# A projection's mask moved into VectorE's gated product, and the roots of its norm chains into one power on GpSimd

## Chip, cores and metric

The kernel runs on one core of a Trainium2 chip. The metric is device time in microseconds (us) of one execution; the median of three runs is given. The engines are TensorE (PE in the profile, its weight loads PEld), VectorE (DVE), ScalarE (ACT), GpSimd (POOL) and SyncE (SP, which here only issues DMAs).

## What is computed

A triangle-style pair update on a 192 x 192 grid with 128 channels, followed by a mixture of experts on the 36,864 tokens. The change touches only the first part, the projections:

```python
zn, pp, lp, ip = (_ln(t, ln_g, ln_b) for t in (z, protein_pair, l_pair, inter_pair))   # norms over 128 channels
gate_proj = lambda x, Wg, bg, W, b: sigmoid(x @ Wg + bg) * (x @ W + b)                  # 128 -> 64
ab1 = gate_proj(zn, Wg1, bg1, W1, b1) * z_mask[..., None]
ab2 = gate_proj(zn, Wg2, bg2, W2, b2) * z_mask[..., None]
ab3 = gate_proj(zn, Wg3, bg3, W3, b3) * z_mask[..., None]
pp, lp, ip = gate_proj(pp, 2), gate_proj(lp, 1), gate_proj(ip, 1)     # shortened: weights by number, no mask
block = einsum('bikc,bkjc->bijc', pp, ab1) + einsum('bikc,bjkc->bijc', ab2, lp) + ab3 * ip
```

z is itself the norm of x over its channels. A norm needs the reciprocal root of variance plus a small constant.

## The kernel before

Four phases run one after another: the projection (to about 547 us), the triangle products, a mix with norms, and the feed-forward. In the projection the grid is cut into 12 blocks of 16 rows; a block has 24 tiles of 128 positions x 128 channels for each of four inputs, x, pp, lp and ip. They are worked in four passes: x in 12 groups of two tiles (G = 0 to 11 of a block), pp, lp and ip in six groups of four tiles each (G = 12 to 17, 18 to 23, 24 to 29). Each engine runs its own program over the same 30 groups, and only semaphores tie them.

For a group, VectorE first takes mean and squares of its tiles (`stats_of`, L96, two tiles an instruction). From these a chain of small VectorE steps makes a scale and a shift for each tile (`chain_step`): a variance (L348), a reciprocal root in eight steps (`rsqrt_step`, L102 to L113), the shift (L352) and an addition (L354). There are two chains a block: EARLY holds the 56 tiles of pp, lp and the first third of ip, its steps standing three to a group from G = 4 on; LATE holds the rest of ip and the next block's x, 40 tiles (24 ahead of the first block, 16 in the last), from G = 17 on. Tables (`share_out`) say at which group each statistic and step stands.

Then the tiles are normalized in place three groups ahead of their use (`norm`): ScalarE takes one tile of a group, or two (L555), GpSimd the others (L594): one of an x group, two or three of the rest. TensorE transposes the tiles one group ahead (`turn`, L645), ScalarE copies the transposes out of PSUM (L566), TensorE projects them (L658) into one of three PSUM buffers, ScalarE applies the sigmoid to the gate half (L582, two buffers `sig_a`). In the x pass GpSimd now multiplies the gates by the mask (L615), and VectorE multiplies value by gate (L727); in the other passes VectorE multiplies at once (L733, L737). TensorE may project into a buffer only when the product of three groups before is done, and ScalarE may reuse a gate buffer only after the product of two groups before.

GpSimd also adds in ab3 * ip (`times_ab3`, L604), six a block: four in the ip pass, the last two in G = 0 and 1 of the next block's x pass, behind the mask product of that group. SP issues the loads of the next block's tiles as TensorE has turned the old ones, and the stores of the products: those of ab wait for the last product of the x pass, and the loads of pp for the next block stand behind them in SP's queue.

Of the kernel before, what the change touches and what calls it, by code (L numbers as in the profile page):

```python
# [22 lines left out]
P = 128  # L23
# [152 lines left out]
def setup_parts(nc, d, s, ctx, ps):  # L176
# [69 lines left out]
    def vector(dve):  # L246
# [16 lines left out]
        ins.then_inc(mask_made, 1)  # L263

# [47 lines left out]
CHAIN_STEPS = LN_STEPS + 1  # L312
# [17 lines left out]
share_out(COEFS_A, AT_X + 4, 3, EARLY, 0, range(CHAIN_STEPS))  # L330
share_out(STATS_A, AT_X + 8, 2, 3, 0, range(IP_SPLIT, TPB, 2))
share_out(STATS_A, AT_PP, 3, 0, 1, range(0, TPB, 2))
share_out(COEFS_A, AT_PP + 5, 3, LATE, 1, range(CHAIN_STEPS))
# [4 lines left out]
def chain_step(nc, dve, step, stepped, before, stats, work, parts, rstd, shift, ready):  # L338

    v = nc.vector  # L340
    tiles = stats.shape[1]
    var, t = (work[:, q, 0:tiles] for q in range(2))
    y = rstd
    if step > 0:
        dve.wait_ge(stepped, before + step)
    if step == 0:
        for lo, hi, factor, addend in parts:
            ins = v.tensor_scalar(var[:, lo:hi], stats[:, lo:hi, SQUARES], factor / CH, addend, ALU.mult, ALU.add)  # L348
    elif step < 1 + RSQRT_STEPS:
        ins = rsqrt_step(v, step - 1, y, t, var)  # L350
    elif step == LN_STEPS - 1:
        ins = v.scalar_tensor_tensor(shift, stats[:, :, MEAN], -1.0, y, ALU.mult, ALU.mult)  # L352
    else:
        v.tensor_scalar(shift, shift, 1.0, None, ALU.add).then_inc(ready, 1)  # L354
        return
    ins.then_inc(stepped, 1)
# [37 lines left out]
def project_phase(nc, d, s):  # L394


    with ExitStack() as ctx:
# [5 lines left out]
        work = sb("work_a", [P, 2, EARLY_TILES])  # L403
# [15 lines left out]
        coefs_ready, own, pool_passed = [sem("early_ready"), sem("late_ready")], sem("coef_stepped_a"), sem("pool_passed_a")  # L419
        q_made = sem("q_made")  # L420
        normed_act, normed_pool = sem("normed_act"), sem("normed_pool")
        turned, copied, projected = sem("turned"), sem("copied"), sem("projected")
        gated, masked, multiplied = sem("gated"), sem("masked"), sem("multiplied")
# [25 lines left out]
        def pool_tiles(i, t0, size):  # L449
            return list(range(t0 + act_share(i, t0), t0 + size))  # L450

# [140 lines left out]
        def _(pool):  # L592
# [29 lines left out]
            setup_gpsimd(pool)  # L622
# [1175 lines left out]
```

## Time and profile before

| | us |
|---|---|
| median of three runs (1394.88 to 1396.71) | 1395.43 |
| profiled execution | 1397.95 |
| its span, first to last instruction | 1396.2 |
| TensorE busy (95% of the span) | 1331.0 |
| VectorE / ScalarE / GpSimd busy | 1125.4 / 998.5 / 996.4 |

How the rows further down are read: in a row in order of time stand the start and the length in us, the engine, the line of the code, the operation, output <- input with shapes, and how many instructions are merged in the row; a bracket at the end is the engine's idle time before it and what ended that. "x8" of a projection are the halves of eight records, one group. In a row by stretches stand the stretch, its length, then the busy time of PE, PEld, DVE, ACT and POOL with the number of instructions, the granted clock of TensorE as a share of its upper level, the mean busy share of the DMA engines, and GB/s. In a row of groups stand line, engine, operation, tiles, shapes and count, then the total in us and the mean of one in ns, then the idle time before them and what ended it.

### The profile page before, as it was taken

Reading aid. Unit: us, or ns where it says so; the run is one execution under the profiler, and the core shown is the slowest. Engines: PE = TensorE matmul, PEld = TensorE weight load, DVE = VectorE, ACT = ScalarE, POOL = GpSimd, SP = SyncE. Lnnn points to the kernel's source line nnn. Section 1 sums busy time; section 2 is a strip of 40 time slices with the busy share of each in tenths; the row PEclk is TensorE's granted clock in tenths of the full one; section 3 lists DMA queues with packets and bytes.
Section 4 is the critical chain, followed back from the end, with each engine's and each line's share of the span. In section 5 each row is a group of like instructions: output and inputs, shape, how many; then the busy total and the mean of one; then the engine's idle time right before and its main releaser. Section 6 shows DMA issues by size and latency. Waiting matters only on the chain. (4 is left out here: it accounts for less than half of the span.)

```text
span 1396.2 us, 30985 instructions
## 1 busy us (share of the span) xinstructions
PE 1331.0 (95%) x9880; PEld 1129.6 (81%) x9880; DVE 1125.4 (81%) x2905; ACT 998.5 (72%) x2327; POOL 996.4 (71%) x1559
## 2 busy tenths in 40 slices
PE   6999999999999997999899999799999999999995
PEld 3887788777887777988767777699999999999994
DVE  6878778888888873787798887667888888888897
ACT  3888889888888886555477776346777766777773
POOL 4998999999999998444389888335555555555574
PEclk9999999999999998999999999899999999999998
DMA  9999999999999999888699994311222232222223
GB/s 214 226 256 258 250 248 249 259 262 257 241 251 267 263 238 291 282 303 294 182 298 333 320 320 172 99 37 61 77 76 76 77 89 79 76 76 77 77 61 91
DMA packets 357520, 267.40 MB, mean 192 GB/s; under 512 B 60432, under 2 KB 332722, under 8 KB 357362
## 3 DMA queue, kind: packets, MB, share of 16 engines
q1 hardware_dynamic: 355800, 264.76, 71.2%
q8 instruction: 82, 1.34, 0.4%
q10 hardware_dynamic: 1290, 0.46, 0.2%
q14 instruction: 76, 0.62, 0.2%
q0 software_dynamic: 272, 0.21, 0.1%
HBM read 171.02 MB, written 94.37 MB: 190 GB/s over the span
## 5 line engine op out<-in xcount | busy, mean ns | idle before, releaser
L1539 ACT ACTIVATE hT<-psH_d,b 128x512 f32<-128x512 f32 x288 | 197.4, 689 | 150.5 <-PE psH_d L1579 150.4
L658 PE MATMUL psZ_a<-w_all,xT_a 128*128 128x128 f32 x1728 | 230.2, 276 | 3.6 <-DVE ip_prod L737 2.0
L658 PEld LDWEIGHTS psZ_a<-w_all,xT_a 128*128 128x128 f32 x1728 | 209.8, 192 | 7.0 <-ACT xT_a L566 4.3
L658 PE MATMUL psZ_a<-w_all,xT_block 128*128 128x384 f32 x576 | 213.4, 493 | 0.1
L582 ACT ACTIVATE sig_a<-psZ_a 128x256 f32<-128x256 f32 (+1 forms) x360 | 153.8, 427 | 74.3 <-PE psZ_a L658 52.0
L594 POOL TENSOR_SCALAR shared<-shared,coefs_early 128x128 f32<-128x128 f32 x468 | 204.1, 461 | 0.0
L645 PE MATMUL psT_a<-ident,shared 128*128 128x128 f32 x1152 | 186.1, 274 | 4.6 <-issue 3.1
L1233 DVE TENSOR_SCALAR shared<-shared,coef 128x128 f32<-128x128 f32 x288 | 185.4, 703 | 1.6 <-POOL xh_b L1613 1.6
L645 PEld LDWEIGHTS psT_a<-ident,shared 128*128 128x128 f32 x1152 | 141.0, 142 | 56.1 <-issue 28.5
L1606 POOL TENSOR_TENSOR u_d<-u_d,gamma 128x512 f32<-128x512 f32 x72 | 93.4, 1297 | 128.6 <-ACT u_d L1522 127.3
L1613 POOL TENSOR_TENSOR xh_b<-shared,b 128x512 f32<-128x512 f32 x72 | 93.3, 1296 | 89.9 <-DVE ffn_sum L1675 88.7
L96 DVE BATCH_NORM_STATS2 stats_early<-shared 128x6 f32<-128x256 f32 x336 | 127.0, 420 | 32.0 <-DMA shared<-L_conv_protein_pair_dram 19.8
L615 POOL TENSOR_TENSOR sig_a<-sig_a,mask 128x384 f32<-128x384 f32 x144 | 119.4, 829 | 30.3 <-ACT sig_a L582 30.3
L1561 PE MATMUL psY_d<-w,hT 128*128 128x128 f32 x1152 | 134.5, 275 | 0.0
L1561 PE MATMUL psR<-w,hT 128*128 128x128 f32 x1152 | 134.5, 275 | 0.0
L594 POOL TENSOR_SCALAR shared<-shared,coefs_late 128x128 f32<-128x128 f32 x276 | 124.2, 465 | 12.6 <-DVE coefs_late L354 10.4
L658 PEld LDWEIGHTS psZ_a<-w_all,xT_block 128*128 128x128 f32 x576 | 99.2, 192 | 40.4 <-issue 1.5
L1561 PEld LDWEIGHTS psY_d<-w,hT 128*128 128x128 f32 x1152 | 131.6, 192 | 0.1
L1561 PEld LDWEIGHTS psR<-w,hT 128*128 128x128 f32 x1152 | 131.5, 192 | 0.0
L566 ACT COPY xT_a<-psT_a 128x512 f32<-128x512 f32 x216 | 124.3, 575 | 1.5
L1090 POOL TENSOR_TENSOR x_c<-y_c,shared 128x256 f32<-128x256 f32 x144 | 105.2, 730 | 21.8 <-DVE y_c L1204 17.6
L1577 PE MATMUL psH_d<-xT_high,w_high 128*128 128x512 f32 x288 | 119.5, 415 | 0.1
(221 smaller groups left out, 3063.6 us busy)
## 6 DMA issues: line engine op xcount, KB each, us to landing
shared<-in_x_dram SPq DMA_DIRECT2D x48, 512.0 KB, 6.5
scratch_xT<-xT_block SPq DMA_DIRECT2D x36, 512.0 KB, 5.7
shared<-scratch_xT SPq DMA_DIRECT2D x36, 512.0 KB, 5.6
scratch_x<-x_c SPq DMA_DIRECT2D x36, 512.0 KB, 4.9
shared<-scratch_x SPq DMA_DIRECT2D x36, 512.0 KB, 3.6
shared<-in_x_dram SPq DMA_DIRECT2D x48, 256.0 KB, 5.3
shared<-L_conv_protein_pair_dram SPq DMA_DIRECT2D x24, 512.0 KB, 7.3
shared<-in_L_conv_l_pair_dram SPq DMA_DIRECT2D x24, 512.0 KB, 8.6
```

The costliest lines, as they stand in the source:

```text
L96: return nc.vector.bn_stats(stats.rearrange("p t s -> p (t s)"), two_tiles.rearrange("p t c -> p c t"))
L566: nc.scalar.copy(turned_x(count, i, t0, size), psT[:, count % 2, 0:size * P]).then_inc(copied, 1)
L582: nc.scalar.activation(sig[:, G % 2, 0:size * k * HID].rearrange("p (t c) -> p t c", t=size), z, ACT.Sigmoid).then_inc(gated, 1)
L594: return nc.gpsimd.tensor_scalar(x, x, r, b, ALU.mult, ALU.add)
L615: nc.gpsimd.tensor_tensor(gates, gates, zm, ALU.mult).then_inc(masked, 1)
L645: ins = nc.tensor.transpose(psT[:, count % 2, j * P:j * P + P], tiles_in[i][:, t0 + j, :], s["ident"][:])
L658: ins = nc.tensor.matmul(out, turned_x(G, i, t0, size)[:, j * P:j * P + P], rhs[i], start=True, stop=True)
L1090: nc.gpsimd.tensor_tensor(x2[:, par, 2 * j:2 * j + 2, :], y[:, j % 2], x_in[:, par, 2 * j:2 * j + 2, :], ALU.add).then_inc(x2_made, 1)
L1233: ins = nc.vector.tensor_scalar(s["xh_d"][:, g % 2, i, :], s["x2"][:, t, :], r, b, ALU.mult, ALU.add)
L1539: nc.scalar.activation(hT[:, S % 2, f, :], psH[:, f, :], ACT.Gelu, bias=s["b1"][:, f:f + 1]).then_inc(gelued, 1)
L1561: ins = nc.tensor.matmul(psY[G % 2][:, i * CH:i * CH + CH], hT[:, G % 2, f, i * P:i * P + P], s["w2"][:, f, :], start=(f == 0), stop=(f == ...
L1577: nc.tensor.matmul(psH[:, f, :], high, xT_high[:, G % 2, :], start=True, stop=False)
```

## The change

GpSimd no longer multiplies the gates by the mask. VectorE's product in the x pass becomes two instructions, one for each tile of the group, that multiply the value (PSUM) by the tile's mask column, a scalar for each partition, and by the gate. VectorE waits for the gates alone.

In both chains the eight root steps go. VectorE makes the variance (G = 4 or G = 17), GpSimd raises it to the power -0.5 in one instruction behind its norms of G = 5 or G = 18, for which it waits for the variance, and VectorE makes shift and addition at G = 6 or G = 19, for which it waits for the root. The chain ahead of the first block is made in the same way.

```diff
-CHAIN_STEPS = LN_STEPS + 1
+CHAIN_STEPS = 3
+ROOT_AT = {5: EARLY, 18: LATE}
...
-share_out(COEFS_A, AT_X + 4, 3, EARLY, 0, range(CHAIN_STEPS))
+share_out(COEFS_A, AT_X + 4, 1, EARLY, 0, range(1))
+share_out(COEFS_A, AT_X + 6, 2, EARLY, 0, range(1, CHAIN_STEPS))
...
-def chain_step(nc, dve, step, stepped, before, stats, work, parts, rstd, shift, ready):
+def chain_step(nc, dve, step, stepped, before, rooted, roots, stats, var, parts, rstd, shift, ready):
...
-    elif step < 1 + RSQRT_STEPS:
-        ins = rsqrt_step(v, step - 1, y, t, var)
-    elif step == LN_STEPS - 1:
-        ins = v.scalar_tensor_tensor(shift, stats[:, :, MEAN], -1.0, y, ALU.mult, ALU.mult)
+        ins.then_inc(stepped, 1)
+    elif step == 1:
+        dve.wait_ge(rooted, roots)
+        v.scalar_tensor_tensor(shift, stats[:, :, MEAN], -1.0, rstd, ALU.mult, ALU.mult).then_inc(stepped, 1)
...
+            def root(n, chain, chains):
+                lo, hi = chain_tiles(n, chain)
+                pool.wait_ge(own, 2 * chains + 1)
+                nc.gpsimd.tensor_tensor(chain_coefs[chain][:, 0, lo:hi], variances[chain][:, lo:hi],
+                                        minus_half[:].broadcast_to([P, hi - lo]), ALU.pow).then_inc(rooted, 1)
+
             def body(n, last):
                 for G, (i, g, t0, size) in enumerate(GROUPS_A):
                     norm(wait, op, normed_pool, n, G, pool_tiles, last)
-                    if i == 0:
-                        pool.wait_ge(gated, NG_A * n + G + 1)
-                        gates = sig[:, G % 2, 0:size * 3 * HID].rearrange("p (t c) -> p t c", t=size)
-                        zm = s["mask"][:, bass.ds(TPB * n + t0, size)].unsqueeze(2).broadcast_to([P, size, 3 * HID])
-                        nc.gpsimd.tensor_tensor(gates, gates, zm, ALU.mult).then_inc(masked, 1)
-
+                    if G in ROOT_AT:
+                        chain = ROOT_AT[G]
+                        root(n + (chain == LATE), chain, 2 * n + 1 + (chain == LATE))
...
-                    if i == 0:
-                        dve.wait_ge(masked, (TPB // 2) * n + g + 1)
-                    else:
-                        dve.wait_ge(gated, NG_A * n + G + 1)
+                    dve.wait_ge(gated, NG_A * n + G + 1)
...
-                        v.tensor_tensor(out, z[:, :, 0:3 * HID].rearrange("p t (g c) -> p t g c", c=CC),
-                                        gate.rearrange("p t (g c) -> p t g c", c=CC), ALU.mult).then_inc(multiplied, 1)
+                        by_group = lambda ap: ap.rearrange("p (g c) -> p g c", c=CC)
+                        for j in range(size):
+                            zm = s["mask"][:, bass.ds(TPB * n + t0 + j, 1)]
+                            ins = v.scalar_tensor_tensor(out[:, j], by_group(z[:, j, 0:3 * HID]), zm, by_group(gate[:, j]),
+                                                         ALU.mult, ALU.mult)
+                        ins.then_inc(multiplied, 1)
```

GpSimd before, from the end of the ip pass into the next x pass (`shared` are the tiles being normalized, `coefs_late` and `coefs_early` the chains' results, `tri` the add-in's output):

```order
L594 TENSOR_SCALAR shared<-shared,coefs_late 128x128
L604 TENSOR_TENSOR tri<-ip_prod,low_ab 128x256
L594 TENSOR_SCALAR shared<-shared,coefs_late 128x128
L615 TENSOR_TENSOR sig_a<-sig_a,mask 128x384
L604 TENSOR_TENSOR tri<-ip_prod,high_ab 128x256
L594 TENSOR_SCALAR shared<-shared,coefs_late 128x128
```

and now, from the same place to the late chain's root in the lp pass:

```order
L611 TENSOR_TENSOR tri<-ip_prod,low_ab 128x256
L601 TENSOR_SCALAR shared<-shared,coefs_late 128x128
L611 TENSOR_TENSOR tri<-ip_prod,high_ab 128x256
L601 TENSOR_SCALAR shared<-shared,coefs_late 128x128
L611 TENSOR_TENSOR tri<-ip_prod,high_ab 128x256
L601 TENSOR_SCALAR shared<-shared,coefs_late 128x128 x4
L618 TENSOR_TENSOR coefs_early<-var_early,minus_half 128x56
L601 TENSOR_SCALAR shared<-shared,coefs_late 128x128 x3
L601 TENSOR_SCALAR shared<-shared,coefs_early 128x128 x27
L618 TENSOR_TENSOR coefs_late<-var_late,minus_half 128x40
```

The mask products are gone from between the norms, and the two roots (L618) stand ahead of three tiles of x and of twelve tiles of lp and ip.

VectorE before, in the x pass from the variance of the early chain on:

```order
L348 TENSOR_SCALAR work_a<-stats_early 128x56 [waits statted_early]
L102 TENSOR_SCALAR coefs_early<-work_a 128x56 [waits coef_stepped_a]
L104 TENSOR_TENSOR work_a<-coefs_early 128x56 [waits coef_stepped_a]
L727 TENSOR_TENSOR low_ab<-psZ_a,sig_a 128x2x24x8 [waits masked]
L106 SCALAR_TENSOR_TENSOR work_a<-work_a 128x56 [waits coef_stepped_a]
L108 SCALAR_TENSOR_TENSOR coefs_early<-work_a,coefs_early 128x56 [waits coef_stepped_a]
```

and now:

```order
L348 TENSOR_SCALAR var_early<-stats_early 128x56 [waits statted_early]
L739 SCALAR_TENSOR_TENSOR low_ab<-psZ_a,mask,sig_a 128x24x8 [waits gated]
L739 SCALAR_TENSOR_TENSOR low_ab<-psZ_a,mask,sig_a 128x24x8
L739 SCALAR_TENSOR_TENSOR low_ab<-psZ_a,mask,sig_a 128x24x8 [waits gated]
L739 SCALAR_TENSOR_TENSOR low_ab<-psZ_a,mask,sig_a 128x24x8
L352 SCALAR_TENSOR_TENSOR coefs_early<-stats_early,coefs_early 128x56 [waits rooted_a]
L355 TENSOR_SCALAR coefs_early<-coefs_early 128x56 [waits coef_stepped_a]
```

The root steps between the products are gone, a product is two instructions, and the shift waits for GpSimd's root with the next products queued behind it.

## Rows read from the trace of the kernel before

**Rows 1.** The page's busy times of the engines over the whole span.
```profile
PE 1331.0 (95%) x9880; PEld 1129.6 (81%) x9880; DVE 1125.4 (81%) x2905; ACT 998.5 (72%) x2327; POOL 996.4 (71%) x1559
```
**Rows 2.** Busy times by stretches, five of the projection's blocks.
```profile
66.82:112.08 45.26, 43.41 (x290) 35.22 (x289) 35.58 (x101) 37.52 (x95) 40.78 (x81) 1.00 1.10 247
...
155.25:200.09 44.84, 43.22 (x291) 35.11 (x289) 34.80 (x100) 37.52 (x95) 40.80 (x81) 1.00 1.05 254
...
243.24:287.28 44.04, 43.15 (x291) 35.18 (x289) 35.49 (x101) 37.52 (x95) 40.68 (x81) 1.00 1.08 251
...
330.44:373.59 43.15, 42.85 (x290) 35.16 (x289) 34.50 (x99) 37.45 (x95) 40.88 (x81) 1.00 1.11 256
...
373.59:417.10 43.51, 42.98 (x290) 35.15 (x289) 35.65 (x103) 37.51 (x95) 40.69 (x81) 1.00 1.08 253
```
**Rows 3.** Order of time, TensorE and GpSimd early in an x pass.
```profile
158.28 1.46 PE L658 MATMUL psZ_a<-w_all,xT_block 128*128 128x384 f32 x4
...
159.78 1.46 PE L658 MATMUL psZ_a<-w_all,xT_block 128*128 128x384 f32 x4
...
160.03 0.74 POOL L604 TENSOR_TENSOR tri<-ip_prod,high_ab 128x256 f32<-128x256 f32 x1
...
160.75 0.45 POOL L594 TENSOR_SCALAR shared<-shared,coefs_late 128x128 f32<-128x128 f32 x1
...
161.27 0.20 PEld L645 LDWEIGHTS psT_a<-ident,shared 128*128 128x128 f32 x2 [0.65 <-ACT shared L555]
...
161.55 1.46 PE L658 MATMUL psZ_a<-w_all,xT_block 128*128 128x384 f32 x4
```
**Rows 4.** Order of time, first groups of a pp pass.
```profile
349.38 1.06 PE L658 MATMUL psZ_a<-w_all,xT_a 128*128 128x128 f32 x8
...
350.61 6.94 POOL L594 TENSOR_SCALAR shared<-shared,coefs_early 128x128 f32<-128x128 f32 x16
...
350.71 1.06 PE L658 MATMUL psZ_a<-w_all,xT_a 128*128 128x128 f32 x8
...
351.14 0.57 ACT L566 COPY xT_a<-psT_a 128x512 f32<-128x512 f32 x1
...
352.03 0.63 PE L645 MATMUL psT_a<-ident,shared 128*128 128x128 f32 x4 [0.26 <-issue]
...
352.49 1.06 PE L658 MATMUL psZ_a<-w_all,xT_a 128*128 128x128 f32 x8
```
**Rows 5.** Groups by line and shape, GpSimd.
```profile
L615 POOL TENSOR_TENSOR sig_a<-sig_a,mask 128x384 f32<-128x384 f32 x144 | 119.4, 829 | 30.3 <-ACT sig_a L582 30.3
...
L1073 POOL TENSOR_SCALAR tri_n<-tri,coefs_c 128x64 f32<-128x64 f32 x144 | 57.1, 397 | 12.2 <-DVE coefs_c L1178 12.2
```
**Rows 6.** Groups by line and shape, VectorE.
```profile
L727 DVE TENSOR_TENSOR low_ab<-psZ_a,sig_a 128x384 f32<-128x384 f32 x96 | 53.0, 552 | 13.7 <-POOL sig_a L615 13.4
...
L106 DVE SCALAR_TENSOR_TENSOR work_a<-work_a 128x56 f32<-128x56 f32 x12 | 7.9, 660 | 0.0
...
L250 DVE SCALAR_TENSOR_TENSOR w_all<-w_raw,ln_g_col,psZ_a 128x512 f32<-128x512 f32 x1 | 0.7, 749 | 0.6 <-PE psZ_a L276 0.6
...
L254 DVE SCALAR_TENSOR_TENSOR ws<-ws_raw,lnc_g_col,psZ_a 64x128 f32<-64x128 f32 x2 | 0.7, 345 | 0.7 <-PE psZ_a L278 0.7
```
**Rows 7.** Order of time, VectorE, the variances of both chains in one block.
```profile
338.90 0.78 DVE L348 TENSOR_SCALAR work_a<-stats_early 128x56 f32<-128x56 f32 x1
...
357.00 0.29 DVE L348 TENSOR_SCALAR work_a<-stats_late 128x16 f32<-128x16 f32 x2
```
**Rows 8.** Order of time, VectorE and TensorE near the end of an lp pass.
```profile
193.09 0.76 DVE L96 BATCH_NORM_STATS2 stats_early<-shared 128x6 f32<-128x256 f32 x2 [1.45 <-DMA shared<-L_conv_protein_pair_dram]
...
194.31 1.13 PE L658 MATMUL psZ_a<-w_all,xT_a 128*128 128x128 f32 x8 [0.87 <-DVE high_lp L733]
...
195.40 0.43 DVE L96 BATCH_NORM_STATS2 stats_early<-shared 128x6 f32<-128x256 f32 x1 [0.56 <-DMA shared<-L_conv_protein_pair_dram]
```
**Rows 9.** Order of time, VectorE behind the first late chain.
```profile
17.82 0.75 DVE L250 SCALAR_TENSOR_TENSOR w_all<-w_raw,ln_g_col,psZ_a 128x512 f32<-128x512 f32 x1 [0.65 <-PE psZ_a L276]
```

More of the change, by code:

```diff
@@ L263, in vector @@
         ins.then_inc(mask_made, 1)
+        dve.wait_ge(mask_made, 1)
     def tensor(pe):
@@ L329 @@
 share_out(STATS_A, AT_X + 2, 2, 3, 0, range(0, IP_SPLIT, 2))
-share_out(COEFS_A, AT_X + 4, 3, EARLY, 0, range(CHAIN_STEPS))
+share_out(COEFS_A, AT_X + 4, 1, EARLY, 0, range(1))
+share_out(COEFS_A, AT_X + 6, 2, EARLY, 0, range(1, CHAIN_STEPS))
 share_out(STATS_A, AT_X + 8, 2, 3, 0, range(IP_SPLIT, TPB, 2))
 share_out(STATS_A, AT_PP, 3, 0, 1, range(0, TPB, 2))
-share_out(COEFS_A, AT_PP + 5, 3, LATE, 1, range(CHAIN_STEPS))
+share_out(COEFS_A, AT_PP + 5, 1, LATE, 1, range(1))
+share_out(COEFS_A, AT_PP + 7, 2, LATE, 1, range(1, CHAIN_STEPS))
 share_out(STATS_A, AT_LP + 4, 3, 1, 1, range(0, TPB, 2))
 share_out(STATS_A, AT_IP + 3, 3, 2, 1, range(0, LP_AHEAD, 2))
-def chain_step(nc, dve, step, stepped, before, stats, work, parts, rstd, shift, ready):
+def chain_step(nc, dve, step, stepped, before, rooted, roots, stats, var, parts, rstd, shift, ready):
     v = nc.vector
[L341 to L345, printed above, removed]
     if step == 0:
@@ L450, in pool_tiles, with chain_tiles @@
             return list(range(t0 + act_share(i, t0), t0 + size))
+        def chain_tiles(n, chain):
+            if chain == EARLY:
+                return 0, EARLY_TILES
+            return IP_TAIL if n == 0 else 0, IP_TAIL if n == NBLK else LATE_TILES
         def all_blocks(body):
@@ L622, in _ @@
             setup_gpsimd(pool)
+            nc.gpsimd.memset(minus_half[:], -0.5).then_inc(half_made, 1)
+            pool.wait_ge(half_made, 1)
+            root(0, LATE, 0)
             for G in (-3, -2, -1):
                 norm(wait, op, normed_pool, 0, G, pool_tiles, False)
-            pool.wait_ge(mask_made, 1)
             all_blocks(body)
@@ L684, in coef_step @@
                     dve.wait_ge(statted[chain], n + 1)
+                lo, hi = chain_tiles(n, chain)
                 if chain == EARLY:
-                    lo, hi, parts = 0, EARLY_TILES, [(0, EARLY_TILES, 1.0, EPS5)]
+                    parts = [(0, EARLY_TILES, 1.0, EPS5)]
                 else:
-                    lo, hi = IP_TAIL if n == 0 else 0, IP_TAIL if n == NBLK else LATE_TILES
                     ends = ((0, IP_TAIL, 1.0, EPS5), (IP_TAIL, LATE_TILES, 1.0 + EPS5, EPS5 * EPS6))
@@ L691, in coef_step @@
                 now = chain_coefs[chain][:, :, lo:hi]
-                chain_step(nc, dve, step, own, LN_STEPS * chains, chain_stats[chain][:, lo:hi], work, parts, now[:, 0], now[:, 1],
-                           coefs_ready[chain])
+                chain_step(nc, dve, step, own, 2 * chains, rooted, chains + 1, chain_stats[chain][:, lo:hi], variances[chain][:, lo:hi],
+                           parts, now[:, 0], now[:, 1], coefs_ready[chain])
                 chains += step == CHAIN_STEPS - 1
```

9 lines of the change are left out of this document (5 added, 4 removed).

## The prediction, made before the changed kernel ran

> **What bounds the kernel now.** I read the busy times first: TensorE is busy for 95% of the span and nothing else comes near [rows 1]. The change touches the projection alone, so the second view is the table of its blocks, one stretch per block of 16 rows, each from the first projection of one x pass to that of the next. The granted clock is 1.00, the upper of its two levels, in all of them, and TensorE works 43.0 of 43.2 us in a good block [rows 2]: what can be won is the little time in which it waits. Six of the ten blocks cut this way take 43.15 to 43.18 us; four take 45.26, 44.84, 44.04 and 43.51.
>
> The third view is order of time, to find those waits. An undisturbed x group takes 1.50 us (158.28 to 159.78) [rows 3], an undisturbed group of the other passes 1.33 us (349.38 to 350.71) [rows 4]. Two places of every block are longer, and GpSimd ends both.
>
> First, the group before the fourth of x: 159.78 to 161.55, 1.77 us, 0.25 us too long (the ten such places of the trace read 1.74 to 1.77). The profile names ScalarE as releaser of the weight load at 161.27, but ScalarE's tile was long done; what ended just before, at 161.20, is GpSimd's normalized tile that began at 160.75 [rows 3]. GpSimd was late because a mask product of 0.83 us and an add-in of 0.74 us stood before it on its engine.
>
> Second, the second group of pp: 350.71 to 352.49, 1.78 us, 0.45 us too long, in all twelve blocks. The transposes at 352.03 need three tiles of the run that GpSimd starts at 350.61, right behind the last mask product; at 6.94/16 = 0.434 us a tile these end at 351.91 [rows 4].
>
> The rest of a good block's slack has other causes (ScalarE's double tiles at the ends of the x and ip passes) and stays.
>
> **Part one: the mask.** It takes 144 instructions of 0.829 us from GpSimd [rows 5], twelve a block or 9.9 us, and with them the wait for the gate that tied GpSimd to the x groups. Norms then run ahead until coefficients or a root stop them. Both places above are cleared: 11 x 0.25 = 2.75 us (the first block has no add-in there) and 12 x 0.45 = 5.4 us.
>
> VectorE's one product of 0.552 us becomes two of half the columns with a per-partition scalar. That form with a PSUM operand stands in the trace at 128 columns (0.345 us) and 512 (0.749 us) [rows 6]; the line through them gives 0.41 us at 192. Two statistics back to back take 0.76 us where one takes 0.43 [rows 8], so the second begins about 0.1 us before the first's recorded end, and a pair of products takes some 0.73 us. From below it could be 0.60 (two halves of today's product plus one start). I take 0.73. The 0.18 us more per group lies beside TensorE: with two statistics (0.76 us) it makes 1.4 us in a 1.5 us group, and the product starts 0.88 us earlier because no mask stands ahead of it. Its end, for which TensorE's third group after and the stores wait, comes about 0.7 us earlier. Cost on the path: nothing. If that cover were gone, it would be 144 x 0.18 = 26 us.
>
> **Part two: the chains.** Each loses eight VectorE steps and gets one power on GpSimd, 24 or 40 columns in the late chain, 56 in the early. The removed steps fill gaps of VectorE; the longest last 0.66 us [rows 6]. None is waited for by TensorE, so I count no gain here. What is added is a wait on each side: GpSimd waits for the variance with all later tiles queued behind it, and VectorE waits for the root with its products queued behind.
>
> How long may the power last unseen? *Late chain:* the variance is ready 0.29 us after 357.00 [rows 7], at 357.29. Behind the root stand three tiles (1.30 us) for the group whose transposes come just before the projection at 352.49 + 7 x 1.33 = 361.80 [rows 4], so at 361.4. With 0.1 us for the signal, 361.4 - 357.3 - 1.3 - 0.1 leaves 2.7 us. From there to the end of the lp pass GpSimd takes 1.30 us a group against TensorE's 1.33 [rows 4], so a longer root is paid in full, once a block. *Early chain:* the block begins at 330.44 [rows 2]; the variance starts today at 338.90 [rows 7], and would be ready at about 338.6 with products 0.7 us earlier and a shorter step. The tile behind it (0.45 us) is needed for the transposes before group eight, at about 330.44 + 0.23 + 8 x 1.51 - 0.2 = 342.5. That leaves 3.4 us. VectorE's own wait allows more at both places.
>
> What does it last? No power is in this trace. From below: the shortest tensor instruction of GpSimd near this size takes 0.397 us for 64 columns [rows 5]. From above, the eight removed steps as eight such instructions: 3.2 us. One instruction with all their arithmetic would be near 0.7 us: the rows of 64 and 128 columns, 0.397 and 0.45 us [rows 3, 5], give 0.34 us fixed and 0.8 ns a column for two operations, and eight times that over 56 columns is 0.37 us. It is nearest to the lower row, and I take it. All of 0.4 to 2.7 us gives the same sum; at 3.2 us in both chains the late one would cost 0.5 us a block, 6 us in all. A routine can also be longer than any of these, which is the first rival.
>
> **Part three: data that come late.** The four long blocks exceed 43.16 us by 2.10, 1.68, 0.88 and 0.35 us. In them VectorE waits for a pp chunk (1.45 us) and TensorE then for VectorE's product (0.87 us) [rows 8]. The load of that chunk is queued on SP behind the stores of ab, and these wait for the last x product. That product comes 0.83 us earlier against TensorE (the mask's time), while the stretch from there to the statistics gets 0.45 us shorter: about 0.4 us of lateness goes in each, 1.5 us in all. From below this is a loss, if faster blocks crowd the transfers; I put -2 to +5 us.
>
> **Start.** The first late chain ends earlier or later with its root, but VectorE's next step waits for TensorE's folding until 17.82, 0.65 us after today's chain has ended [rows 9]: a root no longer than the eight steps it replaces, and 0.65 us, is hidden, and nothing is won. Behind the projection nothing changes.
>
> **Sum.** 2.75 + 5.4 + 1.5 = 9.7 us. The profiled execution took 1397.95 us (its span of 1396.2 and 1.75 around it) and would take 1388.3; against the median of 1395.43, **1385.7 us**. With part three between its bounds and half of the 0.25 us places kept, the forecast's own range is 1381 to 1390.
>
> **Rivals.**
>
> *The root outlasts its cover (slower).* The power is a software routine longer than 2.7 us for 40 columns or 3.4 us for 56. Every excess is then paid by TensorE twelve times. The 8.2 us of parts one and three's 1.5 us are eaten when the two excesses sum to 0.8 us a block, at about 2.9 us and 3.9 us. At 4.5 and 6.2 us the bill is (1.8 + 2.8) x 12 = 55 us less 9.7: 1441 us. At 3.3 and 4.5 us it is 20 us less 9.7: 1406 us. For it: no row bounds a power, and it is the only work in the kernel that would stand alone in front of three normalized tiles. Against: all of GpSimd's tensor rows cost 1 to 3 ns a column, and it would have to take over 55. The Trainium skill (GPSIMD Engine Reference, section 7, Performance pitfalls for Q7 kernels) says that a chain of dependent fp32 operations costs GpSimd 4 cycles an element on the chain, at 1.2 GHz. By that, an estimate: each dependent step of the routine is 0.19 us at 56 columns, and a routine of over some 16 unhidden steps passes the early chain's cover. No run here shows it.
>
> *Another engine is late in the same places (small gain or none).* ScalarE also does two tiles per group around the start of pp, and the DMA engines move 247 to 256 GB/s in these blocks. If ScalarE holds the pp place, only 2.75 + 1.5 us come back: 1391. If blocks keep the transfers' pace, nothing does: 1395. Against it: ScalarE's copy for the group at 352.49 ends at 351.71 [rows 4], before GpSimd's tiles, and the blocks that move the most per second are the short ones [rows 2].
>
> *More is freed.* All of the 5.0 us of late data go: 1382.
>
> **How the numbers follow.** Forecast 0.62, long root 0.22, another engine 0.12, more freed 0.04. A change of 0.2% (2.8 us) is about what a measurement of this kernel can tell from none. Faster: 0.62 + 0.04 + 0.02 = 0.68. Same: 0.09 of the other engine and 0.02 of a root just over its cover, 0.11. Slower: 0.20 + 0.01 = 0.21. The range runs from 1380 to 1406: left out are the longer roots (0.15) and a little below.
>
> **What would show it.** Right: x groups of 1.51 us throughout, the second pp group at 1.33, good blocks near 42.5 us, GpSimd idle ahead of each root for the variance, roots under 2.7 us. Wrong: VectorE's shift steps waiting for the root, TensorE's transposes waiting in the lp pass, a product pair over 0.85 us that ends the idle time of TensorE or ScalarE, or longer waits for the pp chunks.

## The result, and the profile after

| | before | after |
|---|---|---|
| median of four runs, us | 1396.07 | 1543.36 |
| ratio to before, 95% interval | | 1.106 [1.104, 1.108] |
| profiled execution, its span, us | 1396.2 | 1542.3 |

The change makes the kernel 147 us slower, where 1385.7 us, 10 us faster, was predicted; the time lies far outside the range of 1380 to 1406. The busy times of the page of after, with the line of TensorE's granted clock in 40 slices (tenths of the upper level), answer to [rows 1]:

```profile
PE 1375.9 (89%) x9880; PEld 1162.6 (75%) x9880; DVE 1089.7 (71%) x2849; ACT 999.9 (65%) x2327; POOL 1069.3 (69%) x1441
...
PEclk9899899998999989988998999969999999999998
```

Two things stand in it. GpSimd lost 119.4 us of mask products and is still 73 us busier than in [rows 1]. And TensorE, with the same 9880 matmuls, is busy for 45 us more than before (1331.0): its matmuls have become longer.

The groups by line and shape say what GpSimd does instead (line, engine, operation, tiles, shapes, count, total us, mean ns of one, idle time before and its releaser), with the new product of VectorE and the transposes of TensorE:

```profile
L657 PE MATMUL psT_a<-ident,shared 128*128 128x128 f32 x1152 | 199.1, 288 | 110.8 <-issue 108.9 <-POOL shared L601 1.2 <-DVE mask L262 0.6
...
L618 POOL TENSOR_TENSOR coefs_early<-var_early,minus_half 128x56 f32<-128x56 f32 x12 | 111.1, 9259 | 55.7 <-DVE var_early L348 55.7
...
L618 POOL TENSOR_TENSOR coefs_late<-var_late,minus_half 128x40 f32<-128x40 f32 x11 | 74.1, 6740 | 44.0 <-DVE var_late L348 44.0
...
L739 DVE SCALAR_TENSOR_TENSOR low_ab<-psZ_a,mask,sig_a 128x192 f32<-128x192 f32 x192 | 69.9, 410 | 21.2 <-ACT sig_a L589 17.9
...
L618 POOL TENSOR_TENSOR coefs_late<-var_late,minus_half 128x24 f32<-128x24 f32 x1 | 4.2, 4194 | 7.7 <-DVE var_late L348 7.7
```

The transposes in the kernel before, for comparison:

```profile
L645 PE MATMUL psT_a<-ident,shared 128*128 128x128 f32 x1152 | 186.1, 274 | 4.6 <-issue 3.1
```

One power lasts 9.26 us for 56 columns and 6.74 us for 40. From these two, (9259 - 6740) / 16 = 157 ns a column and 0.44 us fixed; the row of 24 columns (4.19 us) lies on the same line. The prediction had taken 0.7 us. The transposes have 110.8 us of idle time ahead of them, where the row of before has 4.6. The profile names no releaser for it ("issue"), so the order of time has to tell.

Block from 360.48 us, around the early root: start, length, engine, line, what, how many merged, idle time before it.

```profile
367.69 0.19 DVE L348 TENSOR_SCALAR var_early<-stats_early 128x56 f32<-128x56 f32 x1
...
367.97 9.26 POOL L618 TENSOR_TENSOR coefs_early<-var_early,minus_half 128x56 f32<-128x56 f32 x1 [4.13 <-DVE var_early L348]
...
370.06 0.74 DVE L739 SCALAR_TENSOR_TENSOR low_ab<-psZ_a,mask,sig_a 128x192 f32<-128x192 f32 x2 [0.77 <-ACT sig_a L589]
...
371.06 1.46 PE L670 MATMUL psZ_a<-w_all,xT_block 128*128 128x384 f32 x4
377.22 1.36 POOL L601 TENSOR_SCALAR shared<-shared,coefs_late 128x128 f32<-128x128 f32 x3
377.26 0.23 DVE L352 SCALAR_TENSOR_TENSOR coefs_early<-stats_early,coefs_early 128x56 f32<-128x56 f32 x1 [6.46 <-POOL coefs_early L618]
377.82 0.66 PE L657 MATMUL psT_a<-ident,shared 128*128 128x128 f32 x2 [5.30 <-issue]
378.27 2.77 PE L670 MATMUL psZ_a<-w_all,xT_block 128*128 128x384 f32 x4
```

GpSimd is held by the root from 367.97 to 377.22; the x tile queued behind it ends about 0.45 us later, and at 377.82 TensorE's transposes begin, after 5.30 us of nothing. The group behind them then takes 2.77 us where every x group ahead of the wait takes 1.46: the same four matmuls. VectorE waits for the root too (6.46 us, L352), with its next products queued behind, but TensorE does not wait for those here: the projection at 378.27 needs the product of three groups before, which is the one of 370.06. The late root of the same block:

```profile
394.04 6.74 POOL L618 TENSOR_TENSOR coefs_late<-var_late,minus_half 128x40 f32<-128x40 f32 x1 [3.88 <-DVE var_late L348]
...
397.18 1.06 PE L670 MATMUL psZ_a<-w_all,xT_a 128*128 128x128 f32 x8
402.21 0.97 PE L657 MATMUL psT_a<-ident,shared 128*128 128x128 f32 x4 [3.98 <-issue]
402.98 1.91 PE L670 MATMUL psZ_a<-w_all,xT_a 128*128 128x128 f32 x8
```

In the stretches of this block (length, busy time of PE, PEld, DVE, ACT and POOL with instructions, granted clock, DMA share, GB/s) the reason can be read off the granted clock:

```profile
360.48:371.06 10.58, 10.58 (x44) 6.53 (x43) 8.01 (x24) 7.81 (x22) 6.45 (x8) 1.00 0.77 216
371.06:378.27 7.21, 1.91 (x8) 1.06 (x7) 0.98 (x4) 1.99 (x5) 7.21 (x4) 0.78 0.86 257
378.27:387.87 9.60, 9.60 (x42) 6.39 (x42) 6.75 (x21) 6.69 (x17) 9.60 (x23) 0.81 0.33 81
387.87:397.18 9.31, 9.31 (x87) 9.31 (x86) 6.44 (x21) 8.67 (x22) 5.43 (x7) 1.00 0.91 251
397.18:402.98 5.80, 1.82 (x15) 1.66 (x14) 1.10 (x4) 1.76 (x5) 5.80 (x7) 0.95 1.18 239
402.98:405.54 2.56, 2.56 (x14) 2.56 (x14) 0.20 (x1) 1.20 (x3) 2.56 (x7) 0.50 1.13 266
405.54:416.11 10.57, 10.57 (x94) 10.37 (x93) 9.10 (x27) 9.50 (x25) 9.99 (x22) 0.99 0.66 168
```

The second row is the early wait, the fifth the late one. Behind each stands a row in which TensorE is busy all the time at a lower granted clock, 0.81 and 0.50 on the mean. At 0.50, the lower of its two levels, the group at 402.98 takes 1.91 us where the one at 397.18 took 1.06. The Trainium skill (TensorE: Matmul & The Clock Gate, Part 1, The HAM clock gate) says that this clock follows how busy the engine has lately been and falls to half when it idles; the rows agree, with 2.77 against 1.46 us for one group.

### The profile page after: what moved, and what is told of

Same layout as the page of the kernel before. It is cut to its first block and busy times, and to the rows that moved or that the text cites. A ratio compares the mean times of both kernels' runs of the same rounds, so it can differ in the third digit from the quotient of the medians.

```text
span 1542.3 us, 30813 instructions
## 1 busy us (share of the span) xinstructions
PE 1375.9 (89%) x9880; PEld 1162.6 (75%) x9880; DVE 1089.7 (71%) x2849; ACT 999.9 (65%) x2327; POOL 1069.3 (69%) x1441
## 5 line engine op out<-in xcount | busy, mean ns | idle before, releaser
L657 PE MATMUL psT_a<-ident,shared 128*128 128x128 f32 x1152 | 199.1, 288 | 110.8 <-issue 108.9
L657 PEld LDWEIGHTS psT_a<-ident,shared 128*128 128x128 f32 x1152 | 151.2, 151 | 168.7 <-issue 151.1
L670 PE MATMUL psZ_a<-w_all,xT_a 128*128 128x128 f32 x1728 | 240.3, 284 | 0.0
L670 PE MATMUL psZ_a<-w_all,xT_block 128*128 128x384 f32 x576 | 234.3, 533 | 0.1
L670 PEld LDWEIGHTS psZ_a<-w_all,xT_a 128*128 128x128 f32 x1728 | 220.4, 200 | 2.4 <-ACT xT_a L573 2.2
L618 POOL TENSOR_TENSOR coefs_early<-var_early,minus_half 128x56 f32<-128x56 f32 x12 | 111.1, 9259 | 55.7 <-DVE var_early L348 55.7
L670 PEld LDWEIGHTS psZ_a<-w_all,xT_block 128*128 128x128 f32 x576 | 108.9, 211 | 45.5 <-issue 12.1
L96 DVE BATCH_NORM_STATS2 stats_early<-shared 128x6 f32<-128x256 f32 x336 | 123.1, 420 | 0.0
L601 POOL TENSOR_SCALAR shared<-shared,coefs_late 128x128 f32<-128x128 f32 x276 | 120.7, 448 | 0.7 <-DVE coefs_late L355 0.7
L618 POOL TENSOR_TENSOR coefs_late<-var_late,minus_half 128x40 f32<-128x40 f32 (+2 forms) x13 | 81.2, 6248 | 56.5 <-DVE var_late L348 56.5
```

What stands on the lines that cost most here:

```text
L96: return nc.vector.bn_stats(stats.rearrange("p t s -> p (t s)"), two_tiles.rearrange("p t c -> p c t"))
L601: return nc.gpsimd.tensor_scalar(x, x, r, b, ALU.mult, ALU.add)
L618: nc.gpsimd.tensor_tensor(chain_coefs[chain][:, 0, lo:hi], variances[chain][:, lo:hi], minus_half[:].broadcast_to([P, hi - lo]), ALU.pow). ...
L657: ins = nc.tensor.transpose(psT[:, count % 2, j * P:j * P + P], tiles_in[i][:, t0 + j, :], s["ident"][:])
L670: ins = nc.tensor.matmul(out, turned_x(G, i, t0, size)[:, j * P:j * P + P], rhs[i], start=True, stop=True)
```

## Experiments

The first four take the change apart. What each had as its measure is the kernel before, run beside it. A ratio is estimated from all these runs and need not be the quotient of the two medians.

**The mask alone.** The kernel before, with the mask in VectorE's product as in the diff, the root steps left on VectorE.

```diff
-                        nc.gpsimd.tensor_tensor(gates, gates, zm, ALU.mult).then_inc(masked, 1)
...
+                            ins = v.scalar_tensor_tensor(out[:, j], by_group(z[:, j, 0:3 * HID]), zm, by_group(gate[:, j]),
+                                                         ALU.mult, ALU.mult)
```

> The mask is in VectorE's product as in the changed kernel; the roots stay in VectorE's eight steps. Theory (the power's length is the whole loss): parts one and three of the prediction stand, 1396.1 - 9.7 = 1386 us, within 3; the second pp group is at 1.33 us, the x groups at 1.51, no TensorE wait for GpSimd of some microseconds. Rival (VectorE's longer products have a part in the loss): slower than before, above 1400 us, with TensorE or ScalarE waiting for the product pair.

Measured: 1392.2 us beside 1396.2, ratio 0.9962 [0.9947, 0.9978]: faster, by 4 to 5 us, not 10. Two undisturbed blocks of it by stretches:

```profile
237.38:279.85 42.47, 42.47 (x290) 35.21 (x289) 36.00 (x116) 37.32 (x95) 31.29 (x68) 1.00 1.10 260
279.85:322.32 42.47, 42.47 (x291) 35.22 (x289) 34.57 (x111) 37.33 (x95) 31.30 (x69) 1.00 1.10 260
```

Against the 43.15 us of [rows 2] a good block is 0.68 us shorter, and TensorE works in all of it. In this trace the projection gains 9 us: the first transposes of the triangle phase stand at 544.1 us against 553.3. But the median gains half of that. This question is taken up again below.

**An addition for the power.** The changed kernel with one word changed; the roots are thereby left out, so the values that follow are others.

```diff
-                                        minus_half[:].broadcast_to([P, hi - lo]), ALU.pow).then_inc(rooted, 1)
+                                        minus_half[:].broadcast_to([P, hi - lo]), ALU.add).then_inc(rooted, 1)
```

> Both power instructions of the changed kernel become additions of the same shape (the roots are left out: -0.5 is added to the variance), with every wait and place kept. Theory (the power's length): an instruction of some 0.4 us fits both covers, and the time is that of the mask alone, 1386 us within 3. Rival (the added waits between VectorE and GpSimd, not the power's length): the time stays far above 1396 us, near 1543 at the worst. Rival (VectorE's longer products): above 1400 us.

Measured: 1391.8 us, ratio 0.9959 [0.9945, 0.9973]. With every wait and every place as in the changed kernel, the whole loss is gone. The same instruction as an addition, and the whole projection of this kernel as one stretch:

```profile
L618 POOL TENSOR_TENSOR coefs_early<-var_early,minus_half 128x56 f32<-128x56 f32 x12 | 3.3, 278 | 54.6 <-DVE var_early L348 54.6
```
```profile
20.98:535.90 514.92, 511.05 (x3437) 421.20 (x3437) 387.28 (x1147) 446.14 (x1121) 371.73 (x828) 1.00 1.05 256
```

0.28 us against 9.26. So it is the operation, not the form, the operand that is spread over the columns, or the waits. The time also equals that of the mask alone, although VectorE is busy for 35 us less (1091.2 against 1126.3): the removed root steps are worth nothing, as predicted. This kernel is the base for the next ones, since it differs from them in the power alone.

**One power at a time.** The early chain keeps its power and the late one gets the addition, and the other way round; the edit of the first is shown.

```diff
-                                        minus_half[:].broadcast_to([P, hi - lo]), ALU.pow).then_inc(rooted, 1)
+                                        minus_half[:].broadcast_to([P, hi - lo]), ALU.pow if chain == EARLY and chains else ALU.add).then_inc(rooted, 1)
```

> Only the early chain's power (56 columns, 9.26 us) is kept; the late chain's becomes an addition (its roots are left out). Theory (each power is paid by what it exceeds its own cover): 12 waits of 5.8 us are 70 us; with TensorE's lower clock behind each wait as a proportional part of the 38 us left over in the changed kernel, 22 us more: 1386 + 92 = 1478 us; without any clock loss 1456. Rival (what counts is GpSimd's whole work in a block, 47 us with both powers against TensorE's 42.5): with one power it is 40.7 us and fits, so about 1386 us.

> Only the late chain's power (40 columns, 6.74 us) is kept; the early chain's becomes an addition (its roots are left out). Theory (each power is paid by what it exceeds its own cover): 12 waits of 4.3 us are 52 us, with a proportional clock loss 16 us more: 1386 + 68 = 1454 us; without any clock loss 1438. Rival (GpSimd's whole work in a block): 38.2 us fits, so about 1386 us. If the two are independent, this excess and that of the early power alone add up to the 157 us between 1386 and 1543.

Measured: 1484.3 us for the early power, ratio 1.063 [1.061, 1.065], and 1453.7 for the late one, 1.041 [1.040, 1.043]. That is 92.5 and 61.9 us over the base, expected were 92 and 68 over 1386. They add up to 154 against the 152 us of both together. The rival falls: GpSimd is busy for 40.5 of 50.1 us in a block of the early power alone, less than the 42.5 that TensorE needs, and the block is 8 us too long all the same. It is the place that counts, not the sum of GpSimd's work. That block, and then the projections as one stretch, of the early power, of the late one, and of the changed kernel:

```profile
333.00:383.13 50.13, 44.82 (x289) 36.35 (x289) 32.74 (x98) 37.39 (x95) 40.52 (x70) 0.93 0.90 223
```
```profile
21.14:629.43 608.29, 539.44 (x3437) 435.29 (x3437) 386.02 (x1147) 447.21 (x1121) 480.12 (x828) 0.94 0.90 217
```
```profile
21.90:599.73 577.83, 533.75 (x3444) 443.41 (x3444) 386.85 (x1148) 448.81 (x1122) 448.20 (x833) 0.96 0.89 229
```
```profile
21.99:687.12 665.13, 556.12 (x3437) 451.07 (x3437) 385.70 (x1147) 448.99 (x1121) 555.32 (x832) 0.92 0.77 199
```

These rows split the loss. Length less TensorE's busy time is its idle time: 3.9 us in the base, 68.9, 44.1 and 109.0 here. Over the base that is 65, 40 and 105 us of waiting. The busy time, of the same matmuls, grows from 511.1 by 28, 23 and 45 us: that is the clock. For the changed kernel 105 + 45 = 150 us, which is the difference of the two projections, 665.1 - 514.9. Less the 4 us that the rest of the change gives, this is the result.

**TensorE kept busy while it waits.** The changed kernel with idle matmuls ahead of the two waiting places, in a PSUM buffer that is free by then; nobody uses what they write.

```diff
+FILL = {9: 18, 22: 13}
...
+                if count in FILL:
+                    need(pe, multiplied, NG_A * n + count - 3)
+                for _ in range(FILL.get(count, 0)):
+                    spare = psZ[:, (count - 1) % 3, 0, 384:512] if i == 0 else psZ[:, (count - 1) % 3, 1, 0:P]
+                    nc.tensor.matmul(spare, s["ident"][:], w[:, 0:P], start=True, stop=True)
```

> The changed kernel, with 18 matmuls of 128 columns (4.95 us at 0.275 us) put into TensorE's program ahead of the transposes that wait for the early chain, and 13 (3.6 us) ahead of those that wait for the late one; their results are used by nobody. The waits stay. Theory (the part of the loss over the waits is TensorE's lower clock behind an idle stretch): the granted clock stays at 1.00 in the projection and the loss of some 3.1 us a block behind the waits goes, 1543 - 37 = 1506 us. Rival (the groups behind a wait are slow for another reason, such as GpSimd or ScalarE catching up): 1543 us or more, since the matmuls can only cost.

Measured: 1505.0 us, ratio 1.077 [1.075, 1.080]: 38 us faster than the changed kernel, with more work. One early wait in order of time, and the projection as one stretch:

```profile
352.71 1.46 PE L676 MATMUL psZ_a<-w_all,xT_block 128*128 128x384 f32 x4
354.01 4.18 PE L657 MATMUL psZ_a<-w_all,ident 128*128 128x128 f32 x36
359.47 0.41 PE L663 MATMUL psT_a<-ident,shared 128*128 128x128 f32 x2 [1.29 <-issue]
359.72 1.46 PE L676 MATMUL psZ_a<-w_all,xT_block 128*128 128x384 f32 x4
```
```profile
22.01:651.50 629.49, 600.06 (x4181) 507.13 (x4181) 384.46 (x1147) 448.78 (x1121) 557.00 (x832) 0.99 0.83 211
```

The group behind the wait is back at 1.46 us and the granted clock at 0.99. The idle matmuls sum to 87.0 us; without them TensorE is busy for 513 us, 2 more than in the base. The wait itself has not become shorter: 629.5 - 513 - 3.9 = 113 us with the idle matmuls in it, against 105. So the 45 us are the clock, shown by taking it away.

**Fewer columns.** Part of the columns goes through the power, the rest through an addition ahead of it: 40 and 24, then 16 and 12; the edit of the second is shown.

```diff
-                nc.gpsimd.tensor_tensor(chain_coefs[chain][:, 0, lo:hi], variances[chain][:, lo:hi],
-                                        minus_half[:].broadcast_to([P, hi - lo]), ALU.pow).then_inc(rooted, 1)
+                mid = lo + (16, 12)[chain]
+                nc.gpsimd.tensor_tensor(chain_coefs[chain][:, 0, mid:hi], variances[chain][:, mid:hi],
+                                        minus_half[:].broadcast_to([P, hi - mid]), ALU.add)
+                nc.gpsimd.tensor_tensor(chain_coefs[chain][:, 0, lo:mid], variances[chain][:, lo:mid],
+                                        minus_half[:].broadcast_to([P, mid - lo]), ALU.pow).then_inc(rooted, 1)
```

> Only 40 of the early chain's 56 columns and 24 of the late chain's 40 go through the power (6.7 and 4.2 us); the others through an addition of some 0.25 us ahead of it (their roots are left out). Theory (covers of 3.4 and 2.7 us, an excess is paid in full): 3.6 + 1.75 us a block are 64 us over the 1392 of the additions: 1456 us without a clock loss, 1481 with one in proportion to the waits. Rival (a fixed toll for each place where a power stands, whatever its length): as with both powers, 1543 us.

> Only 16 and 12 columns go through the power (2.95 and 2.3 us by 0.157 us a column and 0.44), the others through an addition of some 0.25 us ahead of it (their roots are left out). Theory (covers of 3.4 and 2.7 us): both fit, 1392 us as with additions alone. Rival (covers shorter than the prediction's, or a toll for any power): 12 times the excess, over 1400 us.

Measured: 1459.3 us, ratio 1.044 [1.041, 1.048], and 1392.6 us, 0.9969 [0.9953, 0.9984]. The short powers are free: in that kernel these rows, 2.9 and 2.3 us, lie inside the covers, and its time is that of the base.

```profile
L621 POOL TENSOR_TENSOR coefs_early<-var_early,minus_half 128x16 f32<-128x16 f32 x12 | 34.9, 2907 | 0.0
L621 POOL TENSOR_TENSOR coefs_late<-var_late,minus_half 128x12 f32<-128x12 f32 x13 | 29.6, 2279 | 0.0
```

There is no toll for a power as such. The longer ones came between the two values expected. Their projection:

```profile
22.04:605.43 583.39, 528.93 (x3438) 428.59 (x3437) 384.90 (x1147) 448.19 (x1121) 499.15 (x855) 0.97 0.91 226
```

Here 51 us are waiting over the base and 18 the clock: both terms are real, and both were expected a little too large (64 and 25).

**The root alone.** The mask goes back to GpSimd and VectorE's one product; the powers stay.

```diff
...
+                        nc.gpsimd.tensor_tensor(gates, gates, zm, ALU.mult).then_inc(masked, 1)
...
+                        v.tensor_tensor(out, z[:, :, 0:3 * HID].rearrange("p t (g c) -> p t g c", c=CC),
+                                        gate.rearrange("p t (g c) -> p t g c", c=CC), ALU.mult).then_inc(multiplied, 1)
```

> The mask goes back to GpSimd and VectorE's single product; the powers stay on GpSimd. Theory (each power is paid by what it exceeds its own cover, and the two parts add): the 4 to 5 us that the mask gave are missing, 1543 + 5 = 1548 us. Rival (the time freed by the mask pays a part of the powers): GpSimd then has 40.8 + 16.0 = 56.8 us of work in a block of 43.2, and 12 x 13.5 = 162 us are lost at least: 1558 us, and more with TensorE's clock, up to 1600.

Measured: 1610.4 us, ratio 1.152 [1.150, 1.155]. The two parts do not add: without the mask's part the kernel is 67 us slower, where 5 were expected, and the powers cost 213 us over the kernel before, where they cost 152 over the base. The first theory falls, and the rival's 1558 to 1600 was nearer, though still short. One block by stretches, and rows of GpSimd and TensorE around its two roots:

```profile
395.49:456.94 61.45, 46.53 (x291) 37.77 (x289) 31.17 (x86) 37.77 (x95) 56.80 (x82) 0.89 0.70 180
```
```profile
397.56 0.83 POOL L627 TENSOR_TENSOR sig_a<-sig_a,mask 128x384 f32<-128x384 f32 x1 [2.48 <-ACT sig_a L588]
...
406.13 9.26 POOL L617 TENSOR_TENSOR coefs_early<-var_early,minus_half 128x56 f32<-128x56 f32 x1
406.30 1.46 PE L675 MATMUL psZ_a<-w_all,xT_block 128*128 128x384 f32 x4
415.98 0.66 PE L662 MATMUL psT_a<-ident,shared 128*128 128x128 f32 x2 [8.23 <-issue]
...
419.81 0.83 POOL L627 TENSOR_TENSOR sig_a<-sig_a,mask 128x384 f32<-128x384 f32 x1 [1.48 <-ACT sig_a L588]
...
434.70 6.74 POOL L617 TENSOR_TENSOR coefs_late<-var_late,minus_half 128x40 f32<-128x40 f32 x1
435.47 1.06 PE L675 MATMUL psZ_a<-w_all,xT_a 128*128 128x128 f32 x8
442.91 1.08 PE L662 MATMUL psT_a<-ident,shared 128*128 128x128 f32 x4 [6.38 <-issue]
```

GpSimd has the 56.8 us of work that were worked out, more than TensorE's, and is in fact idle for 4.65 us more, mostly because a mask product must wait for the sigmoid of its group, which waits for TensorE's projection (2.48 and 1.48 us in the rows above). So it comes to both roots later. In the changed kernel GpSimd could run ahead: it is idle for 4.13 us before the early root, for the variance, and that root starts 3.09 us ahead of the last projection that TensorE can do without it (367.97 and 371.06); here it starts 0.17 us ahead of it. For the late root it is 3.14 us there (394.04 and 397.18) and 0.77 here. The waits of TensorE are 8.23 and 6.38 us in place of 5.30 and 3.98, which is 5.3 of the 5.8 us by which this block is longer. So the time freed by the mask pays a part of the powers.

**Where half of the mask's gain went.** The kernel before and the mask alone once more, for a second trace of each (one run each, beside 1402.1 us of before).

> The kernel before, unchanged, for a second trace of it. In the mask-alone trace the projection ended 9.2 us earlier than in the trace of before (first transposes of the triangle phase at 544.1 against 553.3 us), but the phases behind it took 846.8 against 842.9 us. Theory (the phases behind vary from one execution to the next by some 4 us whatever the kernel, and the projection of before does not): projection again to about 553 us, phases behind anywhere from 843 to 848. Rival (the shorter projection makes the later phases longer): the phases behind are 843 us again. Second rival (the four long blocks of before vary from one execution to the next): the projection ends some us earlier, its good blocks again at 43.15 us.

> The mask in VectorE's product with the roots in VectorE's eight steps, once more, for a second trace. Theory (phases behind vary whatever the kernel): good blocks at 42.47 us and the projection to about 544 us again, phases behind anywhere from 843 to 848 us. Rival (the shorter projection makes them longer): about 847 us again.

Measured: 1397.8 us for before, 1398.8 for the mask alone. The first theory holds in part and the second rival too. The phases behind the projection took 842.9 and 846.4 us in the two traces of before, 846.8 and 845.1 in the two of the mask alone: they vary, and not with the kernel. But the projections vary as well, and the 544 us expected for the mask alone did not come again. Before had its triangle phase begin at 553.3 and 549.7 us, the mask alone at 544.1 and 552.0. In the second trace of the mask alone most blocks were long; the longest, with what VectorE's statistics waited for in the whole trace:

```profile
153.05:198.82 45.77, 43.08 (x290) 35.27 (x289) 36.28 (x113) 37.43 (x95) 31.20 (x69) 1.00 1.04 247
```
```profile
DVE stats_early L96 <- DMA shared<-L_conv_protein_pair_dram: 25.8, 28, 1.8
DVE stats_early L96 <- DMA shared<-in_L_conv_l_pair_dram: 15.1, 20, 2.5
```

The pp chunks are late, as in [rows 8], for 25.8 us in this trace and 15.5 in the first one of the mask alone (19.8 and 17.0 in the two of before). Their loads stand in SP's queue behind the stores of ab. So the last two kernels move these stores behind the pp loads, for the mask alone and for the kernel before.

```diff
-                    if i == 0:
+                    if i == 1:
                         store_out(n, 0)
```

> The mask in VectorE's product, the roots in VectorE's eight steps, and in SP's queue the stores of ab stand behind the loads of the next block's pp instead of ahead of them (5.7 us of SP's queue in the second trace of the mask alone, 174.5 to 180.25). Theory (the mask's gain is partly eaten because the pp chunks come late behind these stores): the waits of VectorE for pp chunks go, nearly all blocks are at 42.47 us, and 11 blocks at 0.6 to 1.4 us less give 7 to 15 us: 1378 to 1385 us, ratio 0.987 to 0.992 to the kernel before. Rival (the transfers are at their limit in the projection and the next loads in the queue come late instead): 1392 us as with the mask alone, ratio 0.996.

> The kernel before with the same move in SP's queue alone, the mask still on GpSimd. Theory (late pp chunks make the long blocks): all blocks at 43.15 us; in the two traces of before the eleven blocks sum to 482.1 and 479.5 us against 474.7, so 5 to 7 us less: ratio 0.995 to 0.9965. Rival (other loads come late instead): ratio 1.0.

Measured: 1386.5 us beside 1397.05 for the mask alone with the stores moved, ratio 0.9939 [0.9924, 0.9953], the best of all kernels here. It is a little less than expected (0.987 to 0.992). The whole projection of it, and the only wait of VectorE's early statistics for data that is left:

```profile
21.37:531.44 510.07, 510.07 (x3437) 421.62 (x3437) 426.19 (x1339) 446.22 (x1121) 369.98 (x804) 1.00 1.04 259
```
```profile
DVE stats_early L96 <- DMA shared<-in_L_conv_l_pair_dram: 1.3, 3, 0.8
```

All blocks but the first take 42.46 or 42.47 us, and TensorE is busy for 510.07 of 510.07 us: nothing waits any more. So the late pp chunks behind the ab stores are what took the rest of the mask's gain, and the rival (the next loads come late instead) falls for this kernel. The kernel before with the stores moved is at 1395.0 us, 0.9988 [0.9977, 1.0000]. All its blocks but the first (44.92) take 43.12 to 43.14 us, as expected, and its triangle phase begins at 546.5. But in this trace that phase took 135 us, against 131 to 133 in all others, and of the 5 to 7 us expected some 2 are left in the median. Whether the triangle phase is longer in every execution of it, and why, stays open.

With the stores moved in both kernels, the mask gives 8.4 us in the medians (1395.0 - 1386.5), 6.8 by the beginning of the triangle phase in the two traces (546.5 against 539.7), and 0.66 in every block behind the first. What late data cost in single traces scatters: over the eleven blocks with the stores moved, the two traces of before have 6.0 and 3.3 us more and the two of the mask alone 3.7 and 12.5. That the mask made them later is thus seen in one trace of two; that moving the stores sets the mask's gain free rests on the medians.

## Why the prediction was wrong

**What bounds the kernel, and the two places.** Right. TensorE's waits were found where they were, and the mask's part cleared both: in the mask alone the first ten x groups of a block keep a spacing of 1.51 to 1.54 us (block from 237.38 us), and the second group of pp has 1.33:

```profile
257.42 1.06 PE L652 MATMUL psZ_a<-w_all,xT_a 128*128 128x128 f32 x8
...
258.75 1.06 PE L652 MATMUL psZ_a<-w_all,xT_a 128*128 128x128 f32 x8
```

**Part one, the mask.** Right in every term. A pair of products takes 0.74 us in order of time where 0.73 was taken, one of them 0.41 us (L739 above) where 0.41 came from the line through [rows 6], and it is hidden. A good block gives 0.68 us against 0.70 predicted, and 42.47 us against "near 42.5". With the stores moved the whole part is 8.4 us against 8.15.

**Part two, the chains: this step failed.** "It is nearest to the lower row, and I take it": 0.7 us for an instruction that takes 9.26 and 6.74. The upper bound, eight instructions of 0.4 us, was none, because it counted the arithmetic of the removed root and not that of a power, which is another computation. No row held one, and the bounds were drawn from rows of multiplications and additions. The lower row was too high as well (an addition of 56 columns takes 0.28 us, the bound was 0.4), but that changes nothing. The working around this number held: the covers were predicted as 3.4 and 2.7 us. From the waiting of one power at a time, 65 us in 12 and 40 us in 11 places, and powers of 9.28 and 6.75 us in these two runs, they are 9.28 - 5.4 = 3.9 and 6.75 - 3.65 = 3.1 us. With the measured lengths in the prediction's own formula the waits come to 12 x (9.26 - 3.4 + 6.74 - 2.7) = 119 us; 105 are there.

**A term that was missing.** A wait was priced at its own length. Behind each of these waits, TensorE runs at the lower clock for a while: 45 us in all, nearly half of the waiting itself. Whoever adds it gets 119 + 45 - 9.7, 154 us over before, where 147 were measured.

**Part two, the removed steps, and the start.** No gain was counted for VectorE's root steps, and there is none (1391.8 us without and 1392.2 with them). The start was put at nothing; the first power, 24 columns in 4.19 us, moved the first projection from 21.31 to 21.99 us, 0.7 us.

**Part three, data that come late.** Wrong for the mask alone: + 1.5 us was predicted, with - 2 to + 5, and some 4 us of the 8 that the blocks give were missing in the median (1392.2 us, where 1396.2 less 8 is 1388), with a spread from trace to trace. That the last x product comes earlier did not help, since the ab stores still stood ahead of the pp loads; moved behind them they cost nothing, and 1386.5 us came out. That this is near 1385.7 bears out the mask's part alone, as it is another kernel. In the changed kernel itself late data play no part: its blocks are 12 us longer, and VectorE's early statistics never wait for data in its trace.

**The rivals.** The one that came true, "the root outlasts its cover", had the right mechanism, the right place and the right points at which it decides, with a chance of 0.22. Its price was too small: 4.5 and 6.2 us were tried, 1441 us. Against it stood that a power "would have to take over 55 ns a column"; it takes 157. (That the other rows cost 1 to 3 ns a column was loose: 0.397 us for 64 columns is 6, most of it the start of the instruction by the prediction's own line; this changes nothing.) What the Trainium skill (GPSIMD Engine Reference, section 7, Performance pitfalls for Q7 kernels) gives, 4 cycles for a dependent fp32 step, can now be set beside a row: 157 ns a column are 188 cycles of 1.2 GHz, an estimate of 47 such steps, where 16 were worked out as the point from which the early cover is passed. No run here shows how the routine is built. "Another engine is late" came true in part for the mask alone, by way of the transfers.

**Range and chances.** The range ended at 1406 us and left out "the longer roots" with 0.15, the only cases that could cost a hundred microseconds. An operation that no row shows, alone on its engine ahead of work that TensorE needs, twelve times, had no upper bound in the trace; then the range has none on that side either.

**Could the root have been put elsewhere on GpSimd?** In a block of the changed kernel GpSimd is busy for 47.05 us, TensorE needs 42.47. So at least 4.6 us a block would be lost even at the best place, 55 us in all; this is worked out, not tried.

## What to carry to other kernels

A new kind of operation has the price of its own row and no other: the time of the code that it replaces, or of cheap operations of the same shape, bounds nothing, and if it stands alone ahead of tiles that the bounding engine waits for, the range has to say so. A wait of TensorE can cost more than its length: here the matmuls behind waits of 4 and 5.3 us ran at the lower clock, while the waits of 0.25 and 0.45 us in the kernel before left it at 1.00 [rows 2]. Look at the granted clock and at the mean of one matmul, not at idle time alone. And a gain on one engine is only kept if the next queue in line, here the stores of SP ahead of the next loads, is not what is late then.

## What the runs showed of the hardware that was not expected

- GpSimd's power on fp32, with the exponent -0.5 on 128 partitions, costs 157 ns a column and 0.44 us fixed: 2.28 us (12 columns), 2.91 (16), 4.19 (24), 6.74 (40), 9.26 (56). An addition of the same form and 56 columns costs 0.28 us.
- 105 us of TensorE's waiting, in two places of each block, cost 45 us more by the clock; 31 useless matmuls a block in these gaps made the kernel 38 us faster.
- The phases behind the projection took from 842.9 to 847.7 us in thirteen of the fourteen traces, though no kernel changes them, and 850.3 in one: differences of 4 us between two single traces mean nothing there.
